# Query stacking by SBUF transfers, and an earlier load for batch 1 of the second attention, in a two-layer cross-attention kernel

## The reference

```python
def _L0_xattn_ref(x, y, ...):            # 16 heads of 8
    q, k, v = jnp.split(x @ w_qkv + b_qkv, 3, axis=-1)
    x = layer_norm(x + mha(q, k, v) @ w_so + b_so, ln_g, ln_b)
    qc = x @ w_q + b_q
    kc = y @ w_k + b_k
    vc = y @ w_v + b_v
    x = layer_norm(x + mha(qc, kc, vc) @ w_co + b_co, ln_g, ln_b)
    h = jax.nn.relu(x @ w1 + b1)
    h = jax.nn.relu(h @ w2 + b2)
    return layer_norm(x + h @ w3 + b3, ln_g, ln_b)

def _L1_xattn_ref(x, context, ...):      # 16 heads of 64
    h = _layernorm(x, gamma, beta)
    Q, K, V = (h @ Wq), (context @ Wk), (context @ Wv)
    attn = jax.nn.softmax(jnp.einsum('bihd,bjhd->bhij', Q, K), axis=-1) * scale
    return x + jnp.einsum('bhij,bjhd->bihd', attn, V).reshape(B, NQ, INNER) @ Wo + bo
```

## Time and profile before

| | us |
|---|---|
| median of 3 runs | 1109.26 |
| lowest and highest run | 1107.14, 1110.64 |
| profiled execution, its own time | 1106.37 |
| span of the profiled execution | 1104.6 |
| PE busy | 1026.3 (93%) |
| DVE busy | 748.1 (68%) |
| ACT busy | 571.4 (52%) |
| POOL busy | 389.8 (35%) |
| link block | 69.2 to 95.2 us of the span |
| first score of the first attention loop | 115.2 us |
| feed-forward block | from 470.2 us |
| second attention loop | from 579.1 us |

### The profile page before, as it was taken

The page is one execution under the profiler, slowest core; times in us unless marked ns, Lnnn a source line. Parts: engine busy times, 40 slices in busy tenths (PEclk is TensorE's granted clock), DMA queues, the critical chain, the costliest instruction groups (busy, mean ns, idle before and its releaser), DMA issues. The chain is left out here.

```text
span 1104.6 us, 31648 instructions
## 1 busy us (share of the span) xinstructions
PE 1026.3 (93%) x12060; PEld 742.5 (67%) x12060; DVE 748.1 (68%) x1409; ACT 571.4 (52%) x1139; POOL 389.8 (35%) x273
## 2 busy tenths in 40 slices
PE   5977899999999999979688999999999999999997
PEld 2552577777777776646325777777777778777786
DVE  4657788887888778321794776777676767767752
ACT  2533577777777776631444544445444444544442
POOL 4821121111211123030105554545455454646542
PEclk9988899999999999989798999999999999999998
DMA  3501544444444443030002111111111111012100
GB/s 105 144 2 70 145 133 135 126 152 140 128 132 139 141 123 91 2 99 1 0 23 76 56 56 38 55 38 39 54 56 54 41 49 51 28 52 56 35 4 4
DMA packets 48461, 79.41 MB, mean 72 GB/s; under 512 B 8802, under 2 KB 35252, under 8 KB 48404
## 3 DMA queue, kind: packets, MB, share of 16 engines
q1 hardware_dynamic: 48404, 78.61, 23.8%
HBM read 51.13 MB, written 21.96 MB: 66 GB/s over the span
## 5 line engine op out<-in xcount | busy, mean ns | idle before, releaser
L1376 ACT ACTIVATE P<-PS 125x448 f32<-125x448 f32 x384 | 207.1, 544 | 270.3 <-PE PS L1285 268.4
L1266 POOL TENSOR_TENSOR Pl<-P 125x896 f16<-125x896 f32 x128 | 229.9, 1801 | 242.3 <-ACT P L1376 242.3
L1014 DVE TENSOR_REDUCE m<-PS 128x1 f32<-128x500 f32 x336 | 220.8, 675 | 120.1 <-PE PS L1005 118.3
L920 DVE TENSOR_REDUCE m_part<-PS 128x1 f32<-128x500 f32 x336 | 210.5, 673 | 54.8 <-PE PS L822 53.3
L1301 PE MATMUL PS<-cNh,P 125*128 125x97 f16 x1344 | 198.0, 208 | 0.1
L1303 PE MATMUL PS<-cNh,Pl 125*128 125x97 f16 x1344 | 197.4, 207 | 0.0
L1302 PE MATMUL PS<-cNl,P 125*128 125x96 f16 x1344 | 196.8, 206 | 0.0
L898 ACT ACTIVATE Pb<-PS 125x448 f32<-125x448 f32 x384 | 186.0, 547 | 19.5 <-PE PS L797 18.5
L1302 PEld LDWEIGHTS PS<-cNl,P 125*128 125x128 bf16 x1344 | 131.9, 98 | 25.5 <-issue 0.2
L1301 PEld LDWEIGHTS PS<-cNh,P 125*128 125x128 bf16 x1344 | 131.2, 98 | 15.8 <-issue 3.2
L1283 PE MATMUL PS<-Qh,cTh 110*125 110x448 f16 x384 | 139.0, 362 | 1.3 <-DVE Qh L1452 1.3
(11 more groups left out here) (170 smaller groups left out, 1530.0 us busy)
## 6 DMA issues: line engine op xcount, KB each, us to landing
Kst<-k_halves SPq DMA_DIRECT2D x144, 125.0 KB, 2.8
k_halves<-KH SPq DMA_DIRECT2D x16, 750.0 KB, 3.2
cx<-in_ctx SPq DMA_DIRECT2D x16, 562.5 KB
d_cx<-in_ctx SPq DMA_DIRECT2D x16, 562.5 KB
c_halves<-cHi SPq DMA_DIRECT2D x16, 281.2 KB, 2.6
c_halves<-cLo SPq DMA_DIRECT2D x16, 281.2 KB, 3.0
cTh<-c_halves SPq DMA_DIRECT2D x16, 281.2 KB, 3.0
cTl<-c_halves SPq DMA_DIRECT2D x16, 281.2 KB, 3.8
```

The source lines that it names most:

```text
L920: nc.vector.tensor_reduce(m_part[:, t, part:part + 1], PS[:, 6 + k % 2, 0:SP], AX.X, ALU.max).then_inc(s_reduced, 1)
L1014: nc.vector.tensor_reduce(m21[:, t, part:part + 1], PS[:, S1[k % 2], 0:SP], AX.X, ALU.max).then_inc(n_red, 1)
L1266: nc.gpsimd.tensor_tensor(Pl[:, c % NP], P1[:, c % NP], high, ALU.subtract).then_inc(n_low_p, 1)
L1376: nc.scalar.activation(P1[:, c % NP, half * HALF:(half + 1) * HALF], PS[0:KC, u % 3, 0:HALF], ACT.Exp).then_inc(n_exp, 1)
```

## The change

- `wq3`, `bq3` and their six loads go; `LATER` falls from 25 to 19.
- In the link block PE multiplies by `wq` alone. ACT rounds to `Qall` as before, and DVE makes `Qrest`, what rounding left, in one instruction on 128 rows.
- SP has a part in the link block: eight DMAs copy the four groups of `Qall` to rows 0 to 31 and 32 to 63 of `Q16`, four more copy `Qrest` to rows 64 to 95. They count on `q_in`. POOL waits for `q_in` once, in body(-1) of the first loop, ahead of its first `Qst`.
- The three context steps of the link block follow each other in banks 4, 5 and 2 without waits between them (mode `BESIDE_Q`).
- The feed-forward block's SP part ends with the four loads of batch 1, and body(0) of the second loop no longer issues them.

```diff
-        wq3 = sb("wq3", [D, G, 3, 32])
-        bq3 = sb("bq3", [96, G])
+        Qrest = sb("Qrest", [D, TOK], F16)
...
-            return WB if mode == ONE else banks[k]
+            return (4, 5, 2)[k] if mode == BESIDE_Q else banks[k]
...
-            elif mode == ONE:
-                pe.wait_ge(ct_split, n * 3 + k)
-            elif mode == OPEN:
+            elif mode != LOOP:
                 pass
...
-                for rep in range(3):
-                    sp.dma_start(wq3[:, :, rep, :], w_q.rearrange("d (g r) -> d g r", g=G)).then_inc(later_in, 16)
-                    sp.dma_start(bq3[32 * rep:32 * rep + 32, :], b_q.rearrange("(g r) -> r g", g=G), allow_slow_non_contiguous=True).then_inc(later_in, 16)
...
+            @block.sync
+            def _(sp):
+                sp.wait_ge(a_high, 1)
+                for block_row in range(2):
+                    for g in range(G):
+                        sp.dma_start(Q16[32 * block_row:32 * block_row + 32, g, :], Qall[32 * g:32 * g + 32, :]).then_inc(q_in, 16)
+                sp.wait_ge(a_low, 1)
+                for g in range(G):
+                    sp.dma_start(Q16[64:96, g, :], Qrest[32 * g:32 * g + 32, :]).then_inc(q_in, 16)
...
-                pe.wait_ge(v_kept, 3)
-                for g in range(G):
-                    if g == 2:
-                        pe.wait_ge(a_all_kept, 1)
-                    if g == 3:
-                        pe.wait_ge(a_low, 1)
-                    for half in range(2):
-                        mm = pe.matmul(PS[0:96, A_BANK[g] + half, 0:HALF], wq3[:, g].rearrange("p a b -> p (a b)"),
-                                       T128[:, half * HALF:(half + 1) * HALF], start=True, stop=True)
-                    mm.then_inc(a_q, 1)
-                    if g < NSP:
-                        turn_context(pe, -1, 1, g, mode=ONE)
+                for k in range(NSP):
+                    turn_context(pe, -1, 1, k, mode=BESIDE_Q)
...
-                for g in range(G):
-                    dve.wait_ge(a_high, g + 1)
...
-                    if g < NSP:
-                        split_context(dve, -1, 1, g, mode=ONE)
+                dve.wait_ge(a_high, 1)
+                nc.vector.scalar_tensor_tensor(out=Qrest[:].rearrange("p (h c) -> p h c", h=2), in0=PS[:, 6:8, 0:HALF], scalar=bq[:, 0:1],
+                                               in1=Qall[:].rearrange("p (h c) -> p h c", h=2), op0=ALU.add, op1=ALU.subtract).then_inc(a_low, 1)
+                for k in range(NSP):
+                    split_context(dve, -1, 1, k, mode=BESIDE_Q)
...
+                        if isinstance(i, int) and i < 0:
+                            pool.wait_ge(q_in, 16 * 3 * G)
...
-            if half == 0:
+            if half == 0 and not ahead:
                 wait_for(sp, n_st, (n - 1) * 2 * NC)
...
                 load_halves(sp, -1, 1, 1, g_low)
+                load_halves(sp, 0, 0, 0, ahead=True)
+                load_halves(sp, 0, 0, 1, ahead=True)
...
-                    if inside(i, par, 0) and inside(i, par, 1):
+                    if inside(i, par, 0) and inside(i, par, 1) and not (isinstance(i, int) and i == 0 and par == 0):
                         load_halves(sp, i, par, 0)
```

More of the change, by code:

```diff
@@ L256, in lay_keys @@
                 lay(part)
-        LOOP, ONE, OPEN = range(3)
+        LOOP, BESIDE_Q, OPEN = range(3)
         def work_bank(banks, k, mode):
@@ L445, in _ @@
                     keep_keys(act, -1, 0, k, mode=OPEN)
-        LATER = 25
+        LATER = 19
         def row(k):
@@ L685, in program @@
         a_proj, a_link, a_var, a_root = sem("a_proj"), sem("a_link"), sem("a_var"), sem("a_root")
-        a_normed, a_turned, a_kept, a_kept_act, a_all, a_all_kept, a_q, a_high, a_low = (
-            sem(n) for n in ("a_normed", "a_turned", "a_kept", "a_kept_act", "a_all", "a_all_kept", "a_q", "a_high", "a_low"))
-        A_BANK = (0, 2, 6, 0)
+        a_normed, a_turned, a_kept, a_kept_act, a_all, a_high, a_low, q_in = (
+            sem(n) for n in ("a_normed", "a_turned", "a_kept", "a_kept_act", "a_all", "a_high", "a_low", "q_in"))
         with nc.Block() as block:
+            @block.sync
[7 more added lines that the diff above has]
+                    sp.dma_start(Q16[64:96, g, :], Qrest[32 * g:32 * g + 32, :]).then_inc(q_in, 16)
             @block.gpsimd
             def _(pool):
-                pool.wait_ge(a_all_kept, 1)
+                pool.wait_ge(a_high, 1)
                 lay_queries(pool, -1, 0)
@@ L740, in _ @@
                 act.wait_ge(a_all, 1)
[L741 to L747, removed]
+                nc.scalar.activation(Qall[:].rearrange("p (h c) -> p h c", h=2), PS[:, 6:8, 0:HALF], ACT.Identity, bias=bq[:, 0:1]).then_inc(a_high, 1)
+                for k in range(NSP):
+                    keep_context(act, -1, 1, k, mode=BESIDE_Q)
         with nc.Block() as block:
@@ L983, in program, with load_halves @@
         PIECES1 = [(t, part) for part in range(NSP) for t in range(QT)]
-        def load_halves(sp, i, par, half, queries_made=None):
+        def load_halves(sp, i, par, half, queries_made=None, ahead=False):
             slot, n = (par + 1) % 2, i * 2 + par + 1
             keys, queries = ((cTh, Qh), (cTl, Ql))[half]
-            if half == 0:
+            if half == 0 and not ahead:
                 wait_for(sp, n_st, (n - 1) * 2 * NC)
```

## The result

The changed kernel takes 1103.04 us (median of 7 runs, 1101.33 to 1105.47), the kernel before 1109.04 beside it (7 runs, 1107.14 to 1110.64). The ratio is 0.9952, 95% interval 0.9939 to 0.9965: 5.3 us faster by the ratio, 6.0 by the medians. The forecast was 9.05 less, 1100.2; the time lies in the stated range (1096.5 to 1104.5).

The account below looks back on a forecast made before the run. PE, busy 93% of the span, was taken as the bound. Savings of 4.2 + 3.45 + 1.4 = 9.05 took 1106.37 to 1097.3, and 2.9 more for a median gave 1100.2 us, range 1096.5 to 1104.5.

Parts of the forecast that it names:

- rival A: Whole kernel: all three terms hold within their bounds, 1097.5 to 1101.5 us; chance 0.58.
- B: Link block gives only 1.5 us: SP holds 0.69 per issue, or block end awaits copies' landing; 1102.9; chance 0.18.
- C: Clock: no gain at second loop, more half-clock work at first loop's start, 1.5 us lost; 1103.1; chance 0.14.
- Term 2: Second loop's start: loading batch 1 earlier removes PE's wait for `Qh` at 588.04, 3.45 us.
- Term 3: Second loop's start: half clock covers 3.8 us in place of 6.7 once the gap goes, saving 1.4 us.
- Term 1: Link block: ends with SP's twelve issues at 90.9 in place of 95.17, saving 4.2 us.
- The first loop's start: Half clock there, moved by 4.2 us, may gain or lose 1.5 us; set to zero.
- the last sign of being wrong: First loop: its start still at half clock 5 us on would show the prediction wrong.
- Rival E: Link block's twelve copies land one after another, delaying `Qst` and first scores; 14 us slower, 1123.5; chance 0.03.

Follow-up runs that it names:

- load_only: The kernel before with only the earlier load of batch 1 added, the link block as before; 1103.28 us, ratio 0.9951.
- copies_24: The changed kernel with each of SP's twelve copies followed by a second into a spare tile; 1110.23 us, ratio 1.0014 to the kernel before.
- busy_both_pad: `copies_next` with unread PE matmuls filling both loops' starts, plus 25 tiny ones in the feed-forward block; 1092.22 us, ratio 0.9859 to the kernel before.
- copies_next: The changed kernel with the twelve copies issued as SP's first work in the next block, behind the barrier; 1096.18 us, ratio 0.9891 to the kernel before.
- pad_20: `copies_next` with twenty tiny unread PE matmuls in the feed-forward block; 1134.79 us, ratio 1.0242 to the kernel before.
- busy_second: `copies_next` with unread PE matmuls where PE idles around the second loop's start; 1094.42 us, ratio 0.9867 to the kernel before.
- pad_50: `copies_next` with fifty tiny unread PE matmuls in the feed-forward block; 1096.92 us, ratio 0.9890 to the kernel before.
- issue_cost: The changed kernel with 32 more DMAs in the self-attention block, from SBUF or DRAM, 32 or 128 rows, to time SP's issues; 1112.52 us in one run.

## Why the prediction was right, and where it was off

It was right in direction and range, and two of its three terms held. The third, the link block, gave under half of its forecast. So the time is not in the span of rival A, the forecast (1097.5 to 1101.5; its own bounds reach down to 1097.1), but beside the numbers of B (1102.9) and C (1103.1). Step by step:

- **Term 2** (3.45): right. The wait is gone in the changed kernel and in `load_only`, and no `Pl` took its place.
- **Term 3** (1.4): the stretch shortened by 4.76 in all, less 3.45 leaves 1.3. Half clock ended 4.2 us behind the first score (4.6 taken), though it was there at the score already, not 0.8 later. That the size fits so well is in part luck: with the wait gone, the stretch took 28.58 to 30.00 in six other profiles without the filling, so the term was 0.3 to 1.75.
- **Term 1** (4.2): mis-sized, 1.80. The step that failed is the price of SP's issues. The text said that no row shows an SBUF to SBUF copy. One does: `Qh<-QK` of the second loop copies within SBUF, and I read its row for its landing only. The kernel before, SP's timeline:

```profile
579.78 0.54 SPq L997 DMA_DIRECT2D Qh<-QK  x1
580.36 0.58 SPq L994 DMA_DIRECT2D cTl<-c_halves  x1
580.99 0.54 SPq L997 DMA_DIRECT2D Ql<-QK  x1
```

  `Qh`, with rows of 1792 bytes as the copies have, holds SP until the next issue 0.58 later; the 0.63 behind it is the load of `cTl` from DRAM. Twelve at 0.58 would be 7.0 us; at the measured 0.63 they are 7.6 in place of 5.5, 2.1 of the 2.4 us missing. The rest is the block's end behind SP, 0.84 where 0.47 stood behind DVE before (95.17 to 95.64). Term 2's own text had priced four such issues at 0.6; the number stood there and was not carried over. That SP would be the last engine was right, and `copies_24` shows it one for one. Rival B is what happened at this place (it had 1.5), by its first branch: dear issues, 0.63 where it had 0.69. Its second, a block that waits for the landing, is not seen. The next block's first work, expected near 91.3, came at 95.85, and the first scores, expected near 111, at 115.43: 2.0 us of that is `Qall`'s later start, the rest this term.
- **The first loop's start** (zero): the preparation kept its length, 19.60 and 19.58, in part by luck. Windows of the kernel before, and then of the changed one:

```profile
95.64:100.00 4.36, 3.21 (x8) 0.78 (x9) 3.73 (x7) 0.00 (x0) 3.59 (x5) 0.75 0.52 176
100.00:104.00 4.00, 4.00 (x11) 1.43 (x10) 2.87 (x5) 1.17 (x2) 0.00 (x0) 0.50 0.30 101
104.00:105.00 1.00, 1.00 (x5) 0.29 (x3) 1.00 (x3) 0.00 (x0) 0.00 (x0) 0.69 0.01 3
```

```profile
95.85:100.00 4.15, 3.41 (x7) 0.58 (x8) 3.32 (x6) 0.00 (x0) 3.56 (x5) 0.50 0.54 180
100.00:103.60 3.60, 3.60 (x9) 1.29 (x10) 2.50 (x5) 0.59 (x1) 0.20 (x1) 0.50 0.32 110
103.60:104.80 1.20, 1.20 (x6) 0.44 (x4) 0.98 (x2) 0.59 (x1) 0.00 (x0) 0.78 0.06 25
...
115.43:120.50 5.07, 5.07 (x22) 4.03 (x23) 2.55 (x4) 2.92 (x6) 3.70 (x5) 0.50 0.60 156
120.50:122.00 1.50, 1.50 (x11) 1.27 (x11) 1.22 (x3) 1.20 (x4) 0.00 (x0) 0.77 0.30 123
```

  The changed kernel meets more half clock in its first pieces, 0.50 behind 7.82 us of idle on PE in place of 0.75 behind 2.69, and is 0.4 us later at the first matmul that makes keys (4.49 us behind the first piece in place of 4.08), so DVE alone does not pace the pieces there. From there to some 105 us PE has no gap and is the bound, at half clock in both for most of it; there the changed kernel is back at full clock sooner and regains the 0.4. At full clock throughout (`busy_both_pad`, 1.00 from 87.5 to 115) the preparation takes 17.43, so half clock costs some 2.2 us in both kernels and cancels.

  Behind the first score half clock lasted 5.8 us, in place of 3.0: the last sign of being wrong that the prediction names (5 us) did come. It was a poor sign. In four profiles whose code is the same up to there, half clock lasted 3.1 and 2.9 us (`copies_next`, `pad_20`) or 6.1 (`busy_second`, `pad_50`).
- **The sum**: with 1.80 in place of 4.2 it is 6.65, beside 6.0 measured (3.9 to 6.8 by the interval). Rival C needed a term 3 of zero and falls with it, but its other half, a loss at the first loop, was not settled. The four profiles with SP's copies in the link block have 4.1 to 5.8 us of half clock behind the first score and a first loop 0.3 to 0.7 us longer than before; executions of the same code differ by more. Rival E was far off, POOL was 17 us ahead.

## What to carry to other kernels

When all engines must meet at the end of a block, a part put on an idle queue is still on the path: twelve DMA issues took back 7.6 us of the 9.8 that they replaced, and the same twelve behind the barrier cost nothing, as POOL, their reader, had the time. Price an issue by start-to-start times of the same kind of DMA, and look for that kind everywhere in the trace. Look at the instruction packets on the page after each edit, before believing a loss or a gain: here 85 in place of 40 went with 34 to 39 us.

## What the runs showed of the hardware that I had not expected

- Moving PE's second loop body by 31 to 50 matmul records cost 34 to 39 us, 3% of the kernel, and moving it by 13 or 100 did not. It shows as 85 instruction packets in place of 40 and as PE idle for about 5 us at each jump back, "issue" its releaser, with 5.5 us of work at half clock behind it (`pad_20`). By what rule a position is good was not tried.
- In `issue_cost` an issue of a DMA from SBUF took SP 0.63 us with 32 rows and 0.64 with 128.
- The same stretch of unchanged code (`wso` to `Qall`) takes 15.0 to 15.2 us in some executions and 16.8 to 17.4 in others.
- Half clock behind the first loop's first score lasted 2.9 to 3.1 us in two profiles (`pad_20`, `copies_next`) and 6.1 in two others (`busy_second`, `pad_50`), with the same code up to there.
